# A gated cross-attention block with a mixture of experts on one core: another order of work on five engines, with the second norm and the next probabilities ahead of a step's weight work

## The reference

```
x = x + tanh(g_xattn) * attention(layernorm(x), ctx)      # 16 heads, 8 key/value heads, head size 128
xt = layernorm(x)
probs = softmax(xt @ gate_w.T); weight, idx = top_k(probs, 2)
y = sum over e of combine[:, e] * ((silu(xt @ w1[e].T) * (xt @ w3[e].T)) @ w2[e].T)   # hidden 512
y = y + (silu(xt @ sw1.T) * (xt @ sw3.T)) @ sw2.T                                     # hidden 256
x = x + tanh(g_ffn) * y
```

## Time and profile before

| what | value |
|---|---|
| time, median of 3 runs (lowest to highest) | 271.18 us (270.52 to 271.84) |
| profiled execution: its own time | 273.08 us |
| profiled execution: span of the instructions | 271.3 us |
| mean granted clock of TensorE | 0.957 |
| instructions in the profile | 4800 |

### The profile page before, as it was taken

One profiled execution on the slowest core, in us unless ns is written; L12 is line 12 of the kernel. 1 busy time (PEld: TensorE's weight loads), 2 busy tenths in 40 slices (PEclk: granted clock), 3 DMA queues, 4 the chain that ended last, 5 costly groups with the idle time before them and its releaser, 6 DMA issues.

```text
span 271.3 us, 4800 instructions
## 1 busy us (share of the span) xinstructions
PE 227.8 (84%) x1490; PEld 194.0 (72%) x1490; DVE 148.1 (55%) x352; ACT 119.1 (44%) x225; POOL 131.2 (48%) x121
## 2 busy tenths in 40 slices
PE   3999999989969769757776688989999999998920
PEld 1786777879968659646565567878988889887820
DVE  1399889998848556455636417663433435333210
ACT  3376787386543543454423323334344433433310
POOL 4134311748958567844525552164446465452422
PEclk9999999999999995799999959999999999999995
DMA  7753553121413412420002310032423424332131
GB/s 214 228 150 143 164 185 120 58 58 58 138 24 113 138 33 103 135 80 19 19 22 67 108 54 7 0 60 41 77 39 45 75 41 59 58 50 30 23 39 21
DMA packets 12775, 20.99 MB, mean 77 GB/s; under 512 B 2032, under 2 KB 7664, under 8 KB 12752
## 3 DMA queue, kind: packets, MB, share of 16 engines
q1 hardware_dynamic: 9104, 15.71, 18.4%
q0 software_dynamic: 3648, 4.98, 11.5%
HBM read 16.10 MB, written 4.59 MB: 76 GB/s over the span
## 4 chain that ended last, share of the span: by engine, by line
PE 41%; DMA 23%; issue 10%; ACT 8%; POOL 7%; DVE 7%; POOLq 1%; DVEq 1%; SPq 1%; ACTq 0%
DMA out_dram<-probs,tok 19%; PE bankR L358 5%; PE bankQ L242 4%; PE bankQ L244 4%; PE bankQ L243 4%; PE bankP L242 4%; PE bankP L243 4%; PE bankP L244 4%; POOL reg L1411 3%; DMA raw<-kvq_dram 3%; ACT reg L762 2%; ACT probs L805 2%; POOL rstd L1400 2%; PE bankP L335 2%; DMA probs<-x2d,tok 1%
## 5 line engine op out<-in xcount | busy, mean ns | idle before, releaser
L1438 POOL DMA_INDIRECT out_dram<-probs,tok x19 | 30.1, 1587 | 53.3 <-ACT probs L805 30.6
L1411 POOL TENSOR_TENSOR reg<-raw,reg 128x768 fp32r<-128x768 f32 x16 | 29.3, 1833 | 16.5 <-ACT reg L762 16.5
L242 PE MATMUL bankS<-reg,hT 128*128 x76 | 22.9, 301 | 2.4 <-DVE hT L1200 1.5
L1429 POOL DMA_INDIRECT probs<-x2d,tok x19 | 20.2, 1065 | 5.6 <-issue 5.1
L1379 POOL TENSOR_TENSOR w_lo<-raw,w_hi 128x512 fp32r<-128x512 f32 x8 | 10.4, 1301 | 24.4 <-ACT w_hi L686 24.4
L244 PE MATMUL bankS<-reg,hT 128*128 x76 | 21.4, 281 | 0.0
L243 PE MATMUL bankS<-reg,hT 128*128 x76 | 21.4, 281 | 0.0
L1005 DVE TENSOR_TENSOR PT_lo<-bankR,PT_hi 128x512 fp32r<-128x512 f32 x16 | 10.8, 680 | 18.3 <-ACT PT_hi L734 18.3
L792 ACT CAST hT<-bankR 128x512 fp32r<-128x512 f32 x19 | 11.1, 586 | 20.5 <-PE bankR L550 20.5
L1200 DVE TENSOR_TENSOR hT<-bankR,hT 128x512 fp32r<-128x512 f32 x19 | 13.1, 691 | 10.1 <-ACT hT L792 10.1
L1392 POOL TENSOR_TENSOR probs<-probs,rcp 128x1024 f32<-128x1024 f32 x8 | 15.3, 1910 | 4.3 <-DVE rcp L989 4.3
(11 more groups left out here) (232 smaller groups left out, 727.2 us busy)
## 6 DMA issues: line engine op xcount, KB each, us to landing
raw<-ffn_dram SPq DMA_DIRECT2D x18, 384.0 KB, 3.6
raw<-kvq_dram SPq DMA_DIRECT2D x7, 384.0 KB, 3.3
probs<-wo_dram SPq DMA_DIRECT2D x8, 256.0 KB, 2.7
x_sb<-x_dram SPq DMA_DIRECT2D x1, 1024.0 KB, 6.0
x2d<-xn SPq DMA_DIRECT2D x8, 128.0 KB, 1.7
out_dram<-x_sb SPq DMA_DIRECT2D x8, 128.0 KB, 1.7
probs<-x2d,tok POOLq DMA_INDIRECT x19, 2.9
out_dram<-probs,tok POOLq DMA_INDIRECT x19, 3.8
```

What stands on the lines that cost most here:

```text
L242: eng.matmul(acc, l_hi, r_hi, start=start, stop=False, **kw)
L1411: pool.tensor_tensor(lo, raw[:, (m + 2) % RS, :], hi.bitcast(F32), ALU.subtract).then_inc(wf_lo, 1)
L1429: pool.indirect_dma_start(out=x_blk[:, i % 4, :], out_offset=None, in_=x2d[:, :], in_offset=bass.IndirectOffsetOnAxis(ap=tok[:, i:i + 1], ...
L1438: pool.indirect_dma_start(out=out[:, :], out_offset=bass.IndirectOffsetOnAxis(ap=tok[:, i:i + 1], axis=0), in_=y_blk[:, i % 4, :], in_offs ...
```

## The change

No instruction is added or taken out but for waits. The order changes on PE, ACT, DVE and POOL from the attention loop to the start of the expert loop. In attention, POOL takes `scale_x2(n-1)` ahead of both of a step's weight tiles, which lag the old order by two, and `normal_p(n+2)` between them; ACT takes `normal_x2(n-1)` and `split_p(n+1, 0)` ahead of both weight casts; DVE takes `read_logits(n-2)` ahead of `split_p(n+1, 0)`, but takes `choose(0)` ahead of `read_logits(4)`. In the shared part ACT takes `shared_out(n-3)` ahead of `shared_silu(n)`, PE does `shared_up(0)` between the halves of the last `attend`, DVE moves `list_first`, `settle` and the token copies, POOL gathers between the `add_shared`, and the first gathers wait for four stored tiles instead of eight. `shared_down(7)` moves behind the first `up_block`.

```diff
@@ tensor @@
             places(0)
+            pe.wait_ge(wf_lo, JS)
+            pe.wait_ge(x1_ok, NT - 2)
+            shared_up(0)
             attend(7, 1)
             turn_x2(6)
-
-            pe.wait_ge(wf_lo, JS)
             pe.wait_ge(x1_ok, NT - 1)
-            shared_up(0)
-            gate_logits(6)
             shared_up(1)
             shared_turn(0)
-            turn_x2(7)
+            gate_logits(6)
             shared_up(2)
             shared_turn(1)
+            turn_x2(7)
...
                 up_block(i, e[i])
+                if i == 0:
+                    shared_down(7)
+                    pe.wait_ge(s_out, NT)
@@ scalar @@
                 exponent(n + 2)
+                normal_x2(n - 1)
+                split_p(n + 1, 0)
                 split_w(2 * n + 2)
-                normal_x2(n - 1)
                 split_w(2 * n + 3)
-                split_p(n + 1, 0)
...
             for n in range(3, NT):
+                shared_out(n - 3)
                 shared_silu(n)
-                shared_out(n - 3)
                 shared_split(n - 1)
@@ vector @@
                 reciprocal(n + 2)
+                read_logits(n - 2)
                 split_p(n + 1, 0)
-                read_logits(n - 2)
...
             split_p(7, 0)
+            choose(0)
             read_logits(4)
-            choose(0)
@@ gpsimd @@
-                if i == 0:
+                if i in (0, FIRST):
                     for s in range(2):
-                        pool.wait_ge(x2_st[s], 64)
+                        pool.wait_ge(x2_st[s], 32 if i == 0 else 64)
...
             for n in range(2, 6):
-                split_w(2 * n + 2)
                 scale_x2(n - 1)
-                split_w(2 * n + 3)
+                split_w(2 * n)
                 normal_p(n + 2)
+                split_w(2 * n + 1)
...
-            add_shared(0)
-            add_shared(1)
-            add_shared(2)
-            for i in range(4):
-                gather(i)
+            for n in range(3):
+                add_shared(n)
             for n in range(3, NT):
+                gather(n - 3)
                 add_shared(n)
-            gather(4)
```

More of the change, by code:

```diff
@@ L648, in _ @@
             places(1)
+            e = [expert_of(0)]
+            shared_turn(7)
             turn_block(0)
-            shared_turn(7)
             shared_down(6)
-            e = [expert_of(0)]
-            shared_down(7)
             pe.wait_ge(wf_lo, NM)
-            pe.wait_ge(s_out, NT)
             for i in range(NBLK):
@@ L866, in _ @@
             normal_x2(5)
+            split_p(7, 0)
             split_w(15)
-            split_p(7, 0)
             split_p(7, 1)
-            split_x2(5)
-            split_w(16)
-            normal_x2(6)
             act.wait_ge(lsub_ok, 1)
@@ L877, in _ @@
             act.activation(warm[:, :], mhalf[:, 0:1], ACT.Silu)
+            split_x2(5)
+            normal_x2(6)
+            shared_silu(0)
+            split_w(16)
             split_x2(6)
-            shared_silu(0)
+            shared_silu(1)
             normal_x2(7)
-            shared_silu(1)
+            shared_split(0)
+            shared_silu(2)
+            split_x2(7)
+            shared_split(1)
             split_w(17)
[L884 to L887, removed]
             for n in range(3, NT):
+                shared_out(n - 3)
                 shared_silu(n)
-                shared_out(n - 3)
                 shared_split(n - 1)
             shared_out(NT - 3)
+            shared_split(NT - 1)
             split_block(0)
-            shared_split(NT - 1)
             shared_out(NT - 2)
-            shared_out(NT - 1)
             c = [column_of(0)]
@@ L902, in _ @@
                 silu_block(i)
+                if i == 0:
+                    shared_out(NT - 1)
                 if 0 < i < NBLK - 1:
@@ L1305, in _ @@
             aggregate(6)
+            split_x2(5)
+            settle(0)
+            shared_gate(0)
             read_logits(5)
-            settle(0)
-            spots(0, 0, 2)
-            split_x2(6)
             add_attention(7)
@@ L1313, in _ @@
             aggregate(7)
-            shared_gate(0)
+            list_first()
+            split_x2(6)
+            spots(0, 0, 2)
+            shared_gate(1)
+            shared_split(0)
             read_logits(6)
             spots(0, 2, 4)
-            shared_gate(1)
-            shared_split(0)
+            shared_gate(2)
+            shared_split(1)
             split_x2(7)
             select(0)
-            shared_gate(2)
-            shared_split(1)
+            shared_gate(3)
             read_logits(7)
-            list_first()
-            shared_gate(3)
             shared_split(2)
+            shared_gate(4)
+            shared_split(3)
             read_tokens(0)
@@ L1329, in _ @@
             tokens_of(1)
-            shared_gate(4)
-            shared_split(3)
+            shared_gate(5)
+            shared_split(4)
             tokens_of(2)
             tokens_of(3)
-            shared_gate(5)
-            shared_split(4)
+            shared_gate(6)
+            shared_split(5)
             tokens_of(4)
             choose(1)
-            shared_gate(6)
-            shared_split(5)
-            settle(1)
             shared_gate(7)
             shared_split(6)
+            settle(1)
+            shared_split(7)
+            split_block(0)
             spots(1, 4, 6)
-            split_block(0)
-            shared_split(7)
             for i in range(NBLK):
@@ L1464, in _ @@
             normal_p(1)
+            normal_p(2)
             split_w(2)
-            normal_p(2)
+            scale_x2(0)
+            normal_p(3)
             split_w(3)
-            scale_x2(0)
-            split_w(4)
-            normal_p(3)
-            split_w(5)
             for n in range(2, 6):
-                split_w(2 * n + 2)
                 scale_x2(n - 1)
-                split_w(2 * n + 3)
+                split_w(2 * n)
                 normal_p(n + 2)
+                split_w(2 * n + 1)
+            split_w(12)
+            scale_x2(5)
+            split_w(13)
             split_w(14)
-            scale_x2(5)
+            scale_x2(6)
             split_w(15)
-            scale_x2(6)
+            scale_x2(7)
             split_w(16)
-            scale_x2(7)
             split_w(17)
-            add_shared(0)
-            add_shared(1)
-            add_shared(2)
-            for i in range(4):
-                gather(i)
+            for n in range(3):
+                add_shared(n)
             for n in range(3, NT):
+                gather(n - 3)
                 add_shared(n)
-            gather(4)
             raise_e(1)
```

5 lines of the change are left out of this document (3 added, 2 removed).

## The result

The changed kernel takes **261.28 us** (median of 4 runs, 260.91 to 263.41) against 271.51 for the kernel before (4 runs): a ratio of 0.9631, 95% interval 0.9557 to 0.9706. It is faster, as forecast, by 10.2 us instead of 18.7, and it lies outside the range of 246 to 260. Its profiled execution took 260.91 us, with a span of 259.2. Executions over 1.5% above the fastest of their kernel are in a slower state: times are medians of all executions, ratios and intervals come from the others alone.

What follows compares the result with a forecast made beforehand. PE's expert loop bounds the kernel, so its start sets the time: 19.0 us sooner, less 0.2 in the loop, makes 18.8 off the profiled 273.08. From the median, 271.18 - 18.7 = 252.5 us; range 246 to 260.

Steps and rivals of the forecast that it cites:

- What bounds the kernel: Expert loop is PE's own work and can only start sooner; the 111 us from its start to the end move along.
- Attention, steps 2 to 4: Attention loop: PE becomes the limit at 7.6 us a step instead of 10.1, a gain of 7.6 us.
- Attention, its end: Attention's last step: POOL sets the pace, `turn_x2(5)` at 112.4 instead of 119.23, the gain shrinks to 6.8 us.
- The collision with `choose(0)`: End of attention: `gt` of `choose(0)` waits 0 to 1.8 us for a POOL subtraction; 1.05 us taken.
- From there to the loop: From `turn_x2(5)` at 112.4 to the expert loop: `up_block(0)` starts at 141.0 instead of 160.04, 19.0 us sooner.
- The clock: Behind PE's idle time ahead of `turn_x2(5)`: half clock for 6.0 us loses at most 3.0 us; 2 taken.
- A tile of the shared part: Shared part, between `shared_down` of middle tiles: 2.35 us instead of 3.25.
- In the loop: First expert block: 5.1 us instead of 4.11 with `shared_down(7)` behind `up_block(0)`; a 0.80 wait goes; net -0.2 us.
- the ring costs more and DVE sets the pace: Rival: late weight loads in attention cost 5 us, DVE slows shared tiles by 2.3 more: 257 to 266, chance 0.17.
- Slower: the clock: Rival: pauses ahead of the expert loop leave PE at the lower clock in it; six blocks give 281 us, chance 0.03.
- The other two: Rivals: less lost, and the loop starts sooner but something else holds the end, 268 to 272.5 us, chance 0.03.
- less lost: Rival: no lower clock, port collision or waits at the shared part's end, `choose` sooner: 243 to 248 us, chance 0.13.

Runs made afterwards that it cites:

- the shared part alone: The changed kernel with the old order in the attention loop: 266.59 us, ratio to before 0.984.
- PE kept busy: The changed kernel with 22 matmuls that nothing reads added on PE ahead of `turn_x2(5)`: 258.51 us, ratio to before 0.945.
- the kernel with four edits more: The changed kernel with tile 4's logits ahead of `choose(0)`, tile 5's factors and `shared_up(0)` earlier, POOL's last two weight subtractions behind the first adds: 254.9 us.
- the last kernel: The best order with POOL's waits set one place later and tile 5's logits read ahead of the first gate product: 250.46 us, ratio 0.921.
- the best order: The kernel with four edits more, with POOL waiting for both keep masks, tile 6's factors earlier and tile 5 split earlier: 251.79 us, ratio 0.925.

## Why the prediction was wrong

**What bounds the kernel: right.** The loop's start sets the end. From B1 to the end of the span pass 112.8 us after and 111.6 before (159.72 to 271.3), and between 110.5 and 113.3 in every profile here, so a kernel that reaches B1 sooner ends sooner.

**Attention, steps 2 to 4: right.** 7.65 a step against 7.6. ACT waited for a load once, 1.73 us at 102.55, behind these steps, and no one behind it was late.

**Attention, its end: the path was right**, and that the time is right to 0.02 us (41.02 against 41.0) is luck. The collision with `choose(0)` took 1.5 (1.78 instead of 0.26), the full length of a subtraction and not the 1.05 I took between the ends; the handoffs, counted at 0.5, took some 0.15 (the logits end at 111.11, PE starts at 111.26). The all-or-nothing reading of the rule was the one to take.

**From there to the loop: this step failed**, 35.1 us for 28.3. It named both costs, and mis-sized both. In the profiled execution the miss is 6.6 us (260.91 for 254.3): 6.8 on this way and 1.0 behind B1, less the 1.2 by which T0 came sooner.
- *The collision was priced at one place.* The rule that I used at `choose(0)` holds at `list_first`, at `select` and at `choose(1)` as well. At `list_first` and `choose(1)` it lies on PE's path; `select` alone was not tried. I had laid these out with the shortest durations that rows show, `list_first` at 11 instructions in 1.6 us, `gt` at 0.26, and never asked what POOL does at that moment. With POOL out of the way there (but for the 0.72 in `choose(1)`), the same way takes 4.4 us less.
- *The clock was counted at 2 us, and once.* Its bound of 3.0 took the stretch to be the 6.0 us of the earlier trace rows. Here PE works at 0.50 from 111.26 to 119, some 7.7 us, and that costs 3.1, 1.1 above the count. The second stretch, about 0.9, is part of the 4.4.
- With both removed, T0 to B1 is 68.8 against 69.3 forecast. That is not the forecast come true, since its sum had 2 of clock and 1.05 of collision in it: without the 2, it would be 67.3. The 1.4 or so that are left are spread: 0.5 from T5 to T6, 0.3 from T6 to T7 and 0.6 from T7 to B1, the handoffs that I took as short as rows show them.

**A tile of the shared part: right.** 2.32 us between `shared_down` of middle tiles against 2.35, with no wait for `s_y`.

**In the loop: the place was right, the size was not.** `shared_down(7)` behind `up_block(0)` was to make B1 to B2 5.1 us. Where the clock is at 1.00 there, it takes 5.25 to 5.32, in seven kernels. In the changed kernel it takes 6.75, with a level of 0.55 from 146 to 149 us. The forecast's terms were those of the full level, and it had a row against that: the 4.11 of the earlier trace rows was measured in good part at the lower one, as a window of the kernel before shows (length, PE's busy time, granted clock, DMA share, GB/s):

```profile
160.00:162.50 2.50, 2.50 (x8) 0.50 0.25 72
```

Why that third stretch comes is open. It is missing where POOL's add waits for `choose(1)`, and PE's wait ahead of `places(1)` with it, but also in the profiles of the shared part alone and of PE kept busy, which have that wait of 0.79 unchanged. It costs 1.5 us.

**Of the rivals**, *the ring costs more and DVE sets the pace* gave 259.8 and came nearest in number, by another way than it happened: the loads came in time and the tiles kept 2.32. What it said for itself, "every handoff I priced is the shortest that rows show", was the weakness. *Slower: the clock* was right that pauses bring the lower level to the loop's edge, and wrong that it would stay; the waits in front of it were 0.79, 1.19 and 0.41 us, so "no wait longer than 1.3" was no argument against it. The other two did not come: the time is above *less lost*, and the end moved with the loop's start.

## What to carry to other kernels

When an order is rewritten by hand, lay the two engines that share a resource side by side over the whole stretch, and price the rule at each place where they meet; in these traces a short instruction on the path cost what the long one beside it had left. Order can avoid it: a long subtraction that nobody waits for can be held until the last, not the first, of a run of short instructions is through, and it will then meet the next run, so choose one that nobody waits for either. And a pause of PE can cost twice, in itself and in the slower work behind it: 22 matmuls that nothing reads, put into a pause of 7 us, gave back 3.1 us.

## What the runs showed of the hardware that was not expected

- What a held instruction loses doesn't go by its own length. Behind a subtraction of 1.80 to 1.87 us that had just begun, `col` (5 numbers a row) went from 0.17 to 1.76, `rest` (16) from 0.17 to 1.83, `sel` (256) from 0.42 to 1.94, `spot` (1024) from 1.21 to 2.75. The `gt` of `choose(1)` is the exception, 1.21 beside an add of 0.74. Where POOL ran three subtractions back to back, in the kernel with four edits more, DVE got one turn for each: `gt` 1.74, then `eq` 1.88. Instructions with one input in PSUM ran through at their usual length, such as the lo part of the probabilities in the changed kernel, 0.69 us at 107.16, under POOL's pair from 105.98.
- It goes the other way too. In the kernel before, POOL's `rstd`, one number a row, took 1.54 us at 129.44 under DVE's `spot` (129.34, 1.22 us), and 0.57 elsewhere. No run here moves it.
- There are more such places than the four: with PE kept busy, `slot` of `settle(0)` took 1.74 us, where it took 0.31 in the changed kernel.
- An instruction with a single tensor input in SBUF, `rest` by TENSOR_SCALAR, was held too (0.87 under an add). The Trainium skill, SBUF — State Buffer, section "Who interferes with whom", lists tensor_scalar among the operations that can take the shared pair of ports; the trace agrees.
- How long PE stands idle doesn't alone decide the clock. The wait of 2.78 at 82.00 left it alone before the change and the one of 2.90 at 124.75 did not; in the last kernel the level was 0.66 and 0.77 from 107 to 113 us behind a wait of 2.07, while behind one of 2.06 at the same place the best order stayed at 1.00. What decides it, these runs don't say.
